# Starting a chunk's conversions and maxima in its fourth step instead of its first two

## What is computed

```
scores = (Wh @ a1)[:, None] + (We @ a2)[None, :]       # 4096 x 4096
e = where(scores > 0, scores, ALPHA * scores)           # leaky relu, 0.2 and 0.01
e = where(adj > 0, e, NEG_BIG)                          # adj: int32, 4096 x 4096
attention = softmax(e, axis=1)
h = attention @ V                                       # V: entity_embs, then x
x = layernorm(x + elu(h + x))                           # layer 0
x = layernorm(x + h @ W + bias)                         # layer 1, same adj
```

## Time and profile before

| | |
|---|---|
| median of 3 runs | 660.71 us |
| profiled execution | 661.77 us, span 660.0 us |
| VectorE busy | 575.0 us, 87% |
| ScalarE busy | 516.2 us, 78% |
| TensorE busy | 515.8 us, 78% |
| GpSimd busy | 191.6 us, 29% |
| maxima, L722 | 136 of 2261 ns on the mean |
| conversions, L701 and L506 | 44 of 1428 ns, 20 of 2003 ns |
| ScalarE waiting for lifts | 68.3 us, 70 times |

### The profile page before, as it was taken

One profiled execution on the slowest core, in us unless ns is written; L12 is line 12 of the kernel. 1 busy time (PEld: TensorE's weight loads), 2 busy tenths in 40 slices (PEclk: granted clock), 3 DMA queues, 4 the chain that ended last, 5 costly groups with the idle time before them and its releaser, 6 DMA issues.

```text
span 660.0 us, 14220 instructions
## 1 busy us (share of the span) xinstructions
PE 515.8 (78%) x6038; PEld 230.8 (35%) x6039; DVE 575.0 (87%) x729; ACT 516.2 (78%) x592; POOL 191.6 (29%) x143
## 2 busy tenths in 40 slices
PE   1304779899989799999988318778897898899894
PEld 1202345343443344444454203233333233333341
DVE  3888998999999898888467889989998998899685
ACT  0855998899999996898676227979997899699673
POOL 0110000388028850672083000004311450232240
PEclk9999889899999899999998758999999999999998
DMA  7899885687478727430200000000000001000000
GB/s 165 319 360 334 280 285 210 241 288 257 180 242 291 250 94 287 132 126 2 73 3 18 1 32 1 1 33 1 2 9 33 1 1 33 1 1 18 1 17 9
DMA packets 18631, 76.46 MB, mean 116 GB/s; under 512 B 6552, under 2 KB 8776, under 8 KB 10376
## 3 DMA queue, kind: packets, MB, share of 16 engines
q1 hardware_dynamic: 17560, 74.63, 32.5%
q0 software_dynamic: 256, 0.80, 0.4%
q10 hardware_dynamic: 752, 0.13, 0.1%
HBM read 74.47 MB, written 1.09 MB: 114 GB/s over the span
## 4 chain that ended last, share of the span: by engine, by line
PE 31%; DVE 25%; ACT 20%; issue 14%; DMA 4%; POOL 3%; SPq 1%; POOLq 0%; ACTq 0%; DVEq 0%
PE acc L941 16%; ACT Pm L613 14%; DVE junk L722 12%; PE zps L986 9%; DVE zps L816 8%; PE acc L948 4%; DMA adj_in<-in_adj 4%; ACT zps L605 2%; ACT v L506 2%; SPq L350 1%; DVE v L701 1%; DVE tAB L697 1%; ACT u_row L522 1%; DVE tot L757 0%; DVE tot L753 0%
## 5 line engine op out<-in xcount | busy, mean ns | idle before, releaser
L613 ACT ACTIVATE Pm<-zps,ebias 128x1024 f32<-128x1024 f32 (+1 forms) x320 | 293.4, 933 | 82.6 <-DVE zps L816 68.3
L722 DVE CUSTOM_DVE_ANT_0 junk<-v,u_row 128x2048 int8<-128x2048 int8 (+3 forms) x136 | 304.6, 2261 | 2.0 <-ACT v L506 1.8
L986 PE MATMUL zps<-D,v 128*128 128x128 bf16 x2048 | 173.7, 224 | 56.1 <-DVE D L744 29.1
L986 PEld LDWEIGHTS zps<-D,v 128*128 128x128 fp8e4 x2048 | 118.7, 99 | 216.3 <-issue 87.3
L816 DVE SCALAR_TENSOR_TENSOR zps<-S_row,tau_col,zps 128x1024 f32<-128x1024 f32 (+1 forms) x136 | 142.0, 1050 | 50.6 <-PE zps L986 47.7
L605 ACT ACTIVATE zps<-S_row,ntau_col 128x1024 f32<-128x1024 f32 (+1 forms) x184 | 176.6, 960 | 5.4
L941 PE MATMUL acc<-Pm,X 128*32 128x512 f32 (+1 forms) x1280 | 145.5, 527 | 20.2 <-ACT Pm L613 17.8
L941 PE MATMUL acc<-Pm,VE 128*32 128x512 f32 (+1 forms) x1280 | 148.6, 538 | 8.5 <-ACT Pm L613 3.9
L398 POOL TENSOR_TENSOR tAB<-flag,totW 128x520 f32<-128x520 f32 (+1 forms) x8 | 10.3, 1287 | 282.5 <-issue 138.7
L948 PE MATMUL acc<-Pm,ones 128*32 128x256 f32 (+1 forms) x1280 | 87.8, 347 | 0.0
L948 PEld LDWEIGHTS acc<-Pm,ones 128*32 128x32 f32 x1280 | 43.1, 115 | 72.2 <-issue 62.7
(11 more groups left out here) (147 smaller groups left out, 286.4 us busy)
## 6 DMA issues: line engine op xcount, KB each, us to landing
adj_in<-in_adj SPq DMA_DIRECT2D x64, 1024.0 KB, 5.6
S_row<-S_rows_scratch SPq DMA_DIRECT2D x5, 512.0 KB, 3.7
S_row<-S_rows_scratch SPq DMA_DIRECT2D x3, 256.0 KB, 3.1
u_row<-u_row_scratch SPq DMA_DIRECT2D x3, 256.0 KB, 3.5
out<-tAB SPq DMA_DIRECT2D x3, 256.0 KB, 2.6
S_row<-S_rows_scratch POOLq DMA_DIRECT2D x1, 512.0 KB, 11.1
S_row<-S_rows_scratch POOLq DMA_DIRECT2D x1, 256.0 KB, 8.0
out<-tAB SPq DMA_DIRECT2D x2, 128.0 KB, 2.0
```

The costliest lines, as they stand in the source:

```text
L613: a.activation(Pm[:, k % PB, 0:R(C) * P], zps[:, buf("step", k), 0:R(C) * P], ACT.Exp, bias=ebias[:, int(seeded(k)), J:J + 1])\
L722: d.tensor_tensor_reduce(out=junk[:, at % 2, 0:cols.stop - cols.start], in0=v_bytes[:, rt, cols], in1=u_row[:, cols], scale=1.0, scalar=-3 ...
L986: last = t.matmul(zps[:, buf("step", k), r * P:(r + 1) * P], v[:, chunks[C][1] + r, J * P:(J + 1) * P], D[:, C % 2, r, :], start=(r * P % ...
```

## The change

`halves_at` and `pieces_at` spread their items from step 0 and step 1 of a chunk. Now they begin three steps later, at steps 3 and 4, in all chunks but chunk 0, and are spread over the steps that are left. The last items stay where they were. The way in which chunk 4 prepares chunk 5, an own branch of `pieces_at`, is not touched.

```
+    CLEAR = 3
...
             first, end = max(AHEAD, 2 * chunks[C + 1][1]), 2 * (chunks[C + 1][1] + R(C + 1))
-            return [h for h in range(first, end) if (h - first) * 27 // (end - first) == J]
+            clear = CLEAR if C else 0
+            return [h for h in range(first, end) if clear + (h - first) * (27 - clear) // (end - first) == J]
...
             n = 2 * R(C + 1)
-            return [(i, i // 2, i % 2) for i in range(n) if i * 29 // n + 1 == J]
+            clear = CLEAR if C else 0
+            return [(i, i // 2, i % 2) for i in range(n) if clear + i * (29 - clear) // n + 1 == J]
```

## The result

The changed kernel takes 676.14 us (median of 4 runs, 675.64 to 676.24), the kernel before 661.03 us beside it (4 runs): a ratio of 1.0223, 95% interval 1.0203 to 1.0242, 15.1 us. The forecast was 674.1 us in a range of 667 to 680. The profiled execution has a span of 674.4 us against 660.0.

What follows compares the result with a forecast made beforehand. VectorE's instruction stream was taken to end chunks 1, 2, 6 and 7, and nearly chunk 5. Terms 1.8 + 6.0 + 3.6 + 1.0 + 1.0 = 13.4 us, added to 660.71, gave 674.1 us, range 667.0 to 680.0.

Steps and rivals of the forecast that it cites:

- a slack of 0 and of 0.7: Chunk ends: VectorE's diagonals come last, with no slack in chunks 1, 2, 6 and 7, 0.7 us in chunk 5.
- own sign of being wrong: Chunks 1, 6 or 7: forecast wrong if ScalarE's last exponential ends behind the diagonals; no size given.
- the named wait: Chunk 1: VectorE idles 2.0 us before the lift of step 5; chunk 2: 4.2 us before the first maximum.
- The two large terms: Chunks 2 and 5: VectorE idling at their starts, +6.0 and +3.6 us.
- z(5) came where it was put: Chunk 1: the lift of step 5, its tile turned at about 120.0, VectorE idle 2.0 us before it.
- M0's wait: Chunk 2: first maximum waits 4.2 us for ScalarE's conversion of half 40; term 0 to 8, taken as 6.0.
- wait up to 0.8 us at z(12): Chunk 7: up to 0.8 us of new waiting at the lift of step 12, within the chunk's +1.0.
- ScalarE does not decide anywhere: Rival: ScalarE's gaps for early lifts go in chunks 1, 5, 6, 7; together 9.9 us faster, 650.8 us; chance 0.06.
- Given back later: Rival: only the waits in chunks 2 (4.2) and 5 (3.6) reach the end, 668.5 us; chance 0.16.
- Contention: Rival: two more maxima each in chunks 1, 2, 6, 7 meet GpSimd, 1.0 us each, 682.1 us; chance 0.08.

Runs made afterwards that it cites:

- the opposite move: Kernel before, with two conversions ahead of chunk 1's first lift and the first maximum ahead of the first lift in chunks 6 and 7: 655.90 us, ratio 0.9917.

## Why the prediction was right, step by step

The side, the total and the range held. VectorE's stream was rightly named as the bound, and the opposite move gains where the change lost. Through what it bounds was only in part right. In the changed kernel TensorE waits for the diagonals at the ends of chunks 5, 6 and 7 (3.40, 0.69 and 0.69 us). At the ends of chunks 1 and 2 it doesn't: it works without idle from the score reductions on. In the kernel before it waited for them at none of these ends; they were ready 0.3 to 0.4 us before it came to them, and 1.0 at chunk 5's end. The forecast took them as last, with a slack of 0 and of 0.7, which was near enough. Its own sign of being wrong, ScalarE's last exponential behind the diagonals, came true in chunk 1 (182.80 against 182.27) and by 0.3 us in chunks 6 and 7. It had been true before the change as well (180.03 against 179.89 in chunk 1) and tells nothing.

The price by chunk, from the sum of the forecast and from the profiles:

| chunk | forecast | profile | why |
|---|---|---|---|
| 1 | +1.8 | +2.5 | 0.6 by the named wait, the rest behind TensorE's stall |
| 2 | +6.0 | +5.5 | |
| 3 | 0 | -0.3 | |
| 5 | +3.6 | +3.7 | 0.4 of it the clock |
| 6 | +1.0 | +2.0 | 1.2 of it the clock, after chunk 5's late diagonals |
| 7 | +1.0 | -0.5 | later waits given back, 0.6 less busy |
| 8 | 0 | +1.5 | more waits for tiles |

The nearness of the total is in part luck. The two large terms are right to 0.5 us, but chunks 1, 6, 7 and 8 are off by +0.7, +1.0, -1.5 and +1.5, and these errors nearly cancel.

**Chunk 1** has the right size by another way than forecast. z(5) came where it was put, but VectorE reached it 0.7 us later than forecast and waited 1.26 and not 2.0: 0.63 more than in the profile before, and not 1.8. Further 0.80 are before z(28), 0.39 before the next z(0), and 0.6 are longer busy time. The score reductions released TensorE at the same place in the chunk in both profiles, 58.4 us after the first lift. From there to the next first lift it took 15.44 us against 13.01, in both without idle, but in the changed kernel with the clock at 0.50 up to about 173.9. The forecast had no term for that.

**Chunk 2.** Each idle time came as worked out: 4.17 (4.2) before M0, 1.37 (1.8) before z(5), 0.69 (0.9) before z(2), 2.04 (0.92 + 1.1) before the squares, none before the sums. The step that failed is a bound, the sentence by which M0's wait could be nothing and the term with it 0 "if the order on ScalarE came out otherwise". Without that wait the term is 5.3. VectorE is held by z(5), and the wait for the conversion only lay ahead of it. The term is better worked out as the maxima missing before z(5): three of them, M0 to M2, less the M0 that now fits, which is 4.4, and the waits. TensorE's clock fell here too, behind a stall of 3.03 us for the score reductions (0.50 around 250.8 us), but the diagonals alone, 5.5 us later in the chunk than before, hold its length to within 0.3 us.

**Chunk 5** is right in size and mechanism, though incomplete: with M0 and M1 put back the same loss sat before z(7).

**Chunks 6 and 8** are mis-sized too. The forecast let a late chunk 5 hand on nothing but lateness. It also hands on a stalled TensorE, 3.40 us in place of 0 before, at a lower clock: 1.2 us. For chunk 8 I took TensorE as full and so no cost; VectorE's waits for tiles inside it are 7.2 us in all, against 5.7 before, which is the 1.5.

**Chunk 7** went the other way: I had VectorE wait up to 0.8 us at z(12); it waited 0.65 at z(12) and then not again to the end of the chunk, so that all 1.8 us of later waits came back. The waits in its first steps grew by 1.5 and not 2.0, and VectorE was busy for 0.6 less, which the sum didn't have and no run explains.

**The rivals.** ScalarE does not decide anywhere: it gained its early steps and gave them to longer waits, 5.54 us before the first exponential of chunk 6. "Given back later" is out, since chunk 2 lost more than the named wait. Contention: a maximum takes 2275 ns on the mean, 2261 before (a stretched one is in the earlier trace rows); over 136 that is 1.9 us, and the 44 conversions became 1.7 us faster. The rule on two SBUF inputs that the Trainium skill gives in "SBUF — State Buffer", section "Who interferes with whom", still fits the single row (3.28 us, beside GpSimd's work), but the sum of stretched time did not grow. GpSimd's busy time is the same, 191.6 us; that this is the reason is not shown.

## What to carry to other kernels

An engine that is the bound loses what is taken out from in front of an instruction that has to wait, unless a later wait of its own shrinks by it. Chunks 2 and 5 kept the whole loss, chunk 7 gave it back. So before moving filler work, list for each wait of the bound engine what is queued ahead of it, and from when on that wait can end. If the wait named by the profile is removed, look for the next one in the same engine's order before counting the gain; here 4.17 us became 4.64. Gaps at a stage's boundary (1.0 to 2.5 us here) are the place for such filler: two conversions and two maxima there were worth 0.8%.

One profile is one execution. Before a wait in it enters a sum, look whether the clock was up there: 0.63 us of idle and 0.7 us of chunk 1 were not the kernel's but that execution's.

## What the hardware showed that was not expected

TensorE's clock carried a loss over a chunk boundary: after a stall of 3.40 us it ran at a granted 0.51 for the next 4.65 us, which cost 1.2 us there and 0.4 ahead of it, and 28 idle matmuls bought both back. After a stall of 2.2 us in chunk 8 it stayed at 1.00 in one kernel and fell to 0.66 in another. After one of 2.49 us in chunk 1, with the same instructions, it fell to 0.50 in the profile before and stayed at 1.00 in the kernel with only chunks 3 and 7 changed. After one of 4.4 us in chunk 1 it fell in every profile, but for longer in some. Such falls come in pieces of 0.7 to 1.3 us. They go with the scatter between executions of the kernel before (658.81 to 662.83 in 19 runs): the fastest has a mean granted clock of 0.966, the slowest 0.952.
